# One split and one difference of the second pair of hidden blocks change places on VectorE and GpSimd

## What is computed

```python
x = L0_attn_H
xn = _layernorm(x, axis=-1)
x = x + attn(xn, ...) + ffn(xn, ...)

# attention, 16 heads of 16, phi(x) = elu(x) + 1
kv = einsum('bhnd,bhnv->bhdv', phi(k), v);  k1 = phi(k).sum(axis=2)
out = einsum('bhnd,bhdv->bhnv', phi(q), kv) / clip(sum(phi(q) * k1), 1e-6)
out = layernorm(out @ W_proj.T + b_proj) * gamma + beta + xn

# feed-forward
h = silu(tlin(x, w1_w, w1_s)) * tlin(x, w2_w, w2_s)
h = gelu(tlin(h, h1_w, h1_s))          # 1024 x 1024
h = gelu(tlin(h, h2_w, h2_s))          # 1024 x 1024
return tlin(h, w3_w, w3_s)
```

## Time and profile before

| | |
|---|---|
| median of 3 runs | 1537.55 us (1537.16 to 1538.29) |
| the profiled execution | 1536.99 us |
| its span, first to last instruction | 1535.0 us |
| granted clock of TensorE | 0.997 of full speed |
| TensorE, matmuls | 1510.0 us busy, 98% |
| VectorE | 1145.5 us busy, 75% |
| ScalarE | 936.3 us busy, 61% |
| GpSimd | 464.5 us busy, 30% |

### The profile page before, as it was taken

The page is one execution under the profiler, slowest core; times in us unless marked ns, Lnnn a source line. Parts: engine busy times, 40 slices in busy tenths (PEclk is TensorE's granted clock), DMA queues, the critical chain, the costliest instruction groups (busy, mean ns, idle before and its releaser), DMA issues.

```text
span 1535.0 us, 33247 instructions
## 1 busy us (share of the span) xinstructions
PE 1510.0 (98%) x11026; PEld 1421.1 (93%) x11026; DVE 1145.5 (75%) x2054; ACT 936.3 (61%) x1728; POOL 464.5 (30%) x555
## 2 busy tenths in 40 slices
PE   9989999999999999999999999999999999999997
PEld 6988999989999898999989999899998989999897
DVE  5746877688686877868778786786868778687786
ACT  4345656656666665756657566565666656566563
POOL 2112404234052341513325042340523415134140
PEclk9999999999999999999999999999999999999999
DMA  9897754817447273663737548184472736637264
GB/s 271 276 294 261 254 175 142 278 48 264 158 157 261 79 263 118 204 221 102 242 109 246 178 137 280 50 266 159 150 268 75 265 120 197 227 97 261 96 221 133
DMA packets 92272, 291.83 MB, mean 190 GB/s; under 512 B 7376, under 2 KB 52560, under 8 KB 68944
## 3 DMA queue, kind: packets, MB, share of 16 engines
q0 software_dynamic: 43296, 231.75, 46.1%
q1 hardware_dynamic: 48240, 58.23, 12.0%
q10 hardware_dynamic: 704, 1.45, 0.3%
HBM read 274.62 MB, written 23.07 MB: 194 GB/s over the span
## 4 chain that ended last, share of the span: by engine, by line
PE 86%; DVE 6%; DMA 3%; ACT 2%; issue 2%; POOL 0%; DVEq 0%; ACTq 0%; SPq 0%; POOLq 0%
PE ps L929 48%; PE ps L904 13%; PE ps L1002 7%; PE ps L809 4%; PE ps L810 4%; PE ps L811 4%; DMA weight_set<-in_w_ffn 2%; PE ps L849 2%; DVE values_a L1522 2%; PE ps L860 1%; PE ps L870 1%; DMA weight_blocks<-weight_set 1%; PE ps L819 1%; DVE exp_tmp L1502 1%; ACT gate_ring L1160 1%
## 5 line engine op out<-in xcount | busy, mean ns | idle before, releaser
L929 PE MATMUL ps<-operands_a,hidden_weights 128*128 128x256 f32 x5040 | 645.2, 282 | 7.4 <-DVE operands_a L1530 7.3
L929 PEld LDWEIGHTS ps<-operands_a,hidden_weights 128*128 128x128 f32 x5040 | 615.3, 188 | 12.1 <-DVE operands_a L1530 10.5
L1563 DVE TENSOR_TENSOR partial_sums<-partial_sums,ps 128x512 f32<-128x512 f32 x300 | 204.4, 686 | 157.0 <-PE ps L929 105.1
L1530 DVE TENSOR_TENSOR operands_a<-values_a,operands_a 128x512 fp32r<-128x512 f32 x315 | 234.4, 763 | 35.8 <-POOL values_a L695 23.9
L904 PE MATMUL ps<-xnT,w_ffn 128*128 128x512 f32 x1024 | 253.0, 399 | 0.0
L703 POOL DMA_DIRECT2D hidden_weights<-weight_blocks x236 | 131.0, 555 | 402.3 <-PE ps L929 383.6
L929 PE MATMUL ps<-operands_b,hidden_weights 128*128 128x256 f32 x1680 | 235.0, 282 | 1.9 <-DVE partial_sums L1563 1.6
L904 PEld LDWEIGHTS ps<-xnT,w_ffn 128*128 128x128 f32 x1024 | 188.9, 188 | 41.9
L929 PEld LDWEIGHTS ps<-operands_b,hidden_weights 128*128 128x128 f32 x1680 | 213.7, 188 | 5.7 <-issue 3.0
L1224 ACT ACTIVATE values_out<-partial_sums,vectors 128x256 f32<-128x256 f32 x180 | 81.5, 502 | 98.0 <-DVE partial_sums L1563 98.0
L680 POOL TENSOR_TENSOR values_a<-values_a 128x512 f32<-128x512 f32 x30 | 38.2, 1273 | 340.5 <-DVE values_a L1522 340.5
(11 more groups left out here) (126 smaller groups left out, 2241.5 us busy)
## 6 DMA issues: line engine op xcount, KB each, us to landing
hidden_weights<-weight_blocks POOLq DMA_DIRECT2D x180, 1024.0 KB, 5.2
hidden_weights<-weight_blocks POOLq DMA_DIRECT2D x60, 512.0 KB, 4.0
raw_weights<-weight_blocks SPq DMA_DIRECT2D x48, 272.0 KB, 2.7
hidden_weights<-in_w_ffn POOLq DMA_DIRECT2D x16, 512.0 KB, 9.2
weight_set<-in_w_ffn SPq DMA_DIRECT2D x16, 512.0 KB, 9.3
weight_blocks<-weight_set SPq DMA_DIRECT2D x16, 512.0 KB, 3.0
out_dram<-acc SPq DMA_DIRECT2D x32, 256.0 KB, 2.2
x<-in_H SPq DMA_DIRECT2D x15, 512.0 KB, 5.6
```

The lines of the kernel that those rows point to most:

```text
L929: r = mm(bank[:, m * HT:(m + 1) * HT], ring_weights[:, place, 2 * g + j, m * P:(m + 1) * P], as_used(buf[:, j, slot[block_of_b], part, :]) ...
L1530: v.tensor_tensor(lo_part(group, block), value(group, block), hi_part(group, block).bitcast(F32), ALU.subtract).then_inc(lo_half.sem, 1)
L1563: v.tensor_tensor(scratch[:, dst, :], scratch[:, kept, :], product_bank(s, i), ALU.add).then_inc(add.sem, 1)
```

## The change

Two steps change places with a neighbour, each with its entry in the orders. On VectorE, `lo(t, "G1", "T1")` is written ahead of `normalise(t, 1)` instead of behind it. On GpSimd, `t1(t, "G1")` is written ahead of `t3(t, "G0")` instead of behind it, and the table of the differences follows. Nothing is added or taken away. TensorE, ScalarE and the DMA queue of SyncE keep their order.

```diff
-POOL_T = ("G0T1", "G0T2", "G0T4", "G0T3", "G1T1", "G1T2", "G1T3", "G1T4", "H0T1", "H0T2", "H0T3", "H0T4", "H1T3",
+POOL_T = ("G0T1", "G0T2", "G0T4", "G1T1", "G0T3", "G1T2", "G1T3", "G1T4", "H0T1", "H0T2", "H0T3", "H0T4", "H1T3",
...
                     t4(t, "G0")
+                    t1(t, "G1")
                     t3(t, "G0")
-                    t1(t, "G1")
                     t2(t, "G1")
...
                     gated(t, 7)
+                    lo(t, "G1", "T1")
                     normalise(t, 1)
-                    lo(t, "G1", "T1")
                     swap(t)
```

## The result

| | before | changed |
|---|---|---|
| median | 1538.12 us (7 runs, 1536.53 to 1538.29) | 1542.68 us (7 runs, 1542.2 to 1545.59) |
| profiled execution | 1536.99 us, span 1535.0 | 1542.47 us, span 1540.5 |
| ratio, 95% interval | | 1.0034 (1.0025 to 1.0044) |
| from one tile's product 1 to the next, mean of the loop | 93.29 us | 93.75 us |
| last tile, from product 1 to the end of the program | 78.96 us | 78.02 us |

The changed kernel is 0.34% slower by the ratio of all executions, and its median is 4.6 us higher. Both times per tile are read from the starts of product 1 on TensorE: (1462.49 - 149.93)/14 after, (1456.06 - 149.96)/14 before. The loop pays 14 x 0.46 = 6.4 us, and the last tile gives 0.9 back. That is 5.5 us, which is what the two profiled executions differ by. The profiled execution of the kernel before lies 1.1 us under its median; no row explains that microsecond.

What follows compares the result with a forecast made beforehand. TensorE's matmuls, filling 98% of the span, were taken to bound the kernel. Fourteen loop tiles at +0.38 us less 1.1 in the last tile gave +4.2 us, a median of 1541.8, range 1536.3 to 1555.5.

Steps and rivals of the forecast that it cites:

- likeliest case: Whole kernel: a waiting engine gets the port once the holder is through; +4.2 us, median 1541.8, chance 0.50.
- What bounds, and what is late next: TensorE waits for T1(G1)'s split, 0.53 us a tile; removed, it returns at T2(G1)'s split, only some 0.19 staying.
- wait behind 28 matmuls: TensorE, product 5's last four matmuls: wait for T1(G1)'s split, 0.53 us a tile, would go.
- one behind 44: TensorE, ahead of product 6's last four matmuls: a gap of some 0.9 us, waiting for T2(G1)'s split.
- T1 hardly sooner: GpSimd: T1(G1) waits for `gated(3)`, so it starts at 335.69 instead of 335.76, a gain of 0.07.
- The turns of T3(G0) and T2(G1): VectorE and GpSimd alternate: T3(G0) held to 338.66, T1(G1)'s split to 339.21, T2(G1) to 340.36.
- `swap` and T3(G1): VectorE: `swap` ends 341.94; T2(G1)'s split, held by T3(G1), ends 342.72, 0.57 us later than before.
- Size per tile: Loop tile: TensorE reaches `to_rows` at 343.35 instead of 342.97, +0.38 us a tile over 14 tiles.
- Last tile: Last tile: T1(G1)'s split ends 1458.64 instead of 1461.54, T2(G1)'s 1462.79 instead of 1463.91; -1.1 us.
- The rival that GpSimd keeps the port: GpSimd keeps the port when its next difference is queued; B11(G1)'s split delayed, +1.18 a tile, 1553.7; chance 0.22.
- The faster rival: T3(G0) meets neither split, so holds fall elsewhere; -0.24 us a tile, -5.2 in all, 1532.4; chance 0.13.
- The one with a hold fewer: T2(G1)'s split slips in ahead of T3(G1), ending 342.54; +0.20 us a tile, +1.7, 1539.3; chance 0.10.

Runs made afterwards that it cites:

- VectorE's half alone: Kernel before with only the split of T1(G1) moved ahead of the normalisation, GpSimd's order unchanged: 1537.43 us, ratio 0.9994.
- The halved T3(G0): Changed kernel with T3 of G0 computed for only one of its two blocks of rows, so the output is not the layer's: 1535.43 us, ratio 0.9984.
- The two versions that do all of the work: VectorE's half, T2(G1) steps and product 6's add earlier, T3(G1) waiting; T4(G1) waits for split of T3(G0) or T3(G1), against kernel before: 1533.49 or 1534.37 us.
- third nudged kernel: Kernel before with three small VectorE instructions added in the normalisation's second half, to delay the split of T1(G1): 1570.97 us, ratio 1.0218.
- first nudged kernel: Kernel before with one small VectorE instruction added in the normalisation's second half, to delay the split of T1(G1): 1538.08 us, ratio 1.0000.
- the second: Kernel before with two small VectorE instructions added in the normalisation's second half, to delay the split of T1(G1): 1538.00 us, ratio 0.9999.

## Why the prediction was right

The forecast was 1541.8 against a median of 1537.55, 4.2 us more. Measured are 1542.68 against 1538.12, 4.6 us more; 1542.68 lies within the likeliest case's own range of 1540.5 to 1543.5. (The bounds of 0.30 to 0.46 us a tile with -1.1 for the last tile give 1540.7 to 1542.9; the range was written wider than its terms.) The profiled executions differ by 5.5, so the mechanism cost 1.3 us more than forecast, and part of the closeness of 4.2 to 4.6 is luck.

- **What bounds, and what is late next: right.** The wait behind 28 matmuls went and one behind 44 came. VectorE's half alone shows the claim by itself: TensorE's first wait removed returned at once as a second. I expected 0.19 us a tile to stay in that undisturbed case; 0.07 was lost instead. The step that was wrong is that T1's split, the normalisation and `swap` leave the end of T2(G1)'s split at 342.15 in either order. With this profile's 0.96 taken off it ended at 342.41. Two things lead there at once: the split of T1(G1) holds T2(G1), so T3(G1) ends 0.26 later, which I worked out only for the experiment; and `swap` starts 0.18 later, as told below.
- **T1 hardly sooner: right.** 336.58 - 0.89 = 335.69, as forecast.
- **The turns of T3(G0) and T2(G1): right.** T3(G0) 1.75 (forecast 1.7), split of T1(G1) 1.12 (1.1), ending at 339.21 (339.21). The assumption behind them, that a waiting engine gets in between two queued instructions of the other, had no row for two differences in a row; I chose it at 0.50. It held in all 15 tiles. The halved T3(G0) shows that this hold is the loss.
- **`swap` and T3(G1): one step wrong, without effect on the sum.** I let `swap` follow 1.59 us behind the start of the normalisation. It took 1.78 (340.02 to 341.80): the split that stood between the last product of the normalisation and `swap` had covered the semaphore between these two. So `swap` ended 0.22 later than forecast, and the split of T2(G1) came when T3(G1) had just let go, and was not held (0.68). My chain reached 342.72 by a hold, the kernel 342.76 without one. T3(G1) ended at 342.21, and 0.55 behind that is 342.76 too, so by the same steps an earlier `swap` would not have helped.
- **Size per tile: +0.46 for +0.38.** Of the difference 0.04 is the end of that split; the rest is in the steps at the restart, which I had put together from rows of two tiles.
- **Last tile: -1.1 at `to_rows`, as forecast** (7.40 us behind product 1 for 8.48); to the end of the program 0.9 of it stayed.
- **The rival that GpSimd keeps the port did not come**: no gap behind 12 matmuls and a split of B11(G1) of 1.20, not 2.4. Its ground, the last tile's stall, was real, but belongs to an issue of a DMA ahead of the difference. The faster rival did not come either. The one with a hold fewer did not come in its time: the hold by T3(G1) was not there, but the later `swap` took its place.

## What to carry to other kernels

Before a step is moved in front of a wait, ask which operand the same consumer needs next and whether its chain gets any shorter: here the first wait was worth 0.53 us a tile, and the next one gave all of it back even undisturbed. An idle stretch of an engine can be what lets another run: in GpSimd's 1.37 us idle a two-operand split of VectorE ran free (0.67 in VectorE's half alone), and the two halves of this change, harmless alone (0.06 and 0.07 us a tile), cost 0.46 together. The two versions that do all of the work and were faster than the kernel before (0.9978 and 0.9982) moved the chain as a whole: splits, first parts, the add that frees the bank, and waits that keep GpSimd's differences from a split that is about to come. Which of these steps could be left out was not tried. And before a cost per tile is put down to one wait, look whether all tiles pay it: of the 2.37 us of the third nudged kernel 0.73 were the lower clock in half of the tiles.

## What the runs showed of the hardware

- A VectorE instruction with two SBUF operands and a GpSimd difference exclude each other for their length. If one waits, it gets in between two queued instructions of the other: 15 of 15 tiles, in which T3(G0) and T2(G1) grew from 1.30 to 1.75 us. A held split ended 0.54 to 0.56 us after the difference, a held difference 1.15 to 1.16 after the split. The Trainium skill (SBUF — State Buffer, "Who interferes with whom") gives the exclusion and that the first to issue has it for the whole instruction; the trace agrees.
- Behind the issue of the refill on GpSimd this is different. A split that comes up to 0.129 us after the issue has begun passes (42 of 42); one that comes 0.164 to 0.260 us after it waits for the difference queued behind the issue as well (18 of 18), 2.2 us for 0.67, though that difference begins 0.33 to 0.43 us after it. Ahead of the small L670 a split at 0.50 to 0.52 us passed (11 of 11), so the offset is no rule for every issue. The Trainium skill (SBUF — State Buffer, "Who interferes with whom") has "Whoever issues first gets the shared pair for the whole instruction", which does not give this if the start in the trace is the issue. Whether GpSimd takes the port for the next difference during the DMA issue, or the issue itself holds it and hands it on, these runs don't tell: the issue took 0.57 us either way.
- Small instructions placed ahead of a wait on a semaphore cost nothing until they outlast it: the first two of 128x16 did not move the split later, the third did by 0.05 us.
- After an idle time of 1.97 to 2.02 us TensorE's granted clock fell to half, the 1.2 GHz level, in 8 of the 15 tiles of the third nudged kernel (PEclk 0.50; 4.16 us for 20 matmuls in place of 2.64), and stayed at full in the other seven. Behind 1.98 us in the last tile it fell in the first nudged kernel and stayed in the second and in the kernel before. These runs don't tell what decides.
